# Head sums and the subtraction ahead of the exponent over 1,024 columns, with a shorter warm-up and the last chunk in pieces

## What is computed

```python
x = x + 0.5 * ffn(layernorm(x))
x = x + attention(layernorm(x))
x = x + 0.5 * ffn(layernorm(x))

# ffn: weights with a part that depends on the sequence's first tokens (even and odd rows)
m1 = even[:4] outer odd[:4]; m2 = even[4:] outer odd[4:]       # per sequence
h = gelu(x @ (W1 + scale * m1).T + b1);  out = h @ (W2 + scale * m2).T + b2

# attention: 16 heads of 8 features
def feature_map(x, R):
    x = x / sqrt(8)
    return exp(x @ R - 0.5 * sum(x * x, axis=-1))              # one sum per head
q1, k1 = feature_map(q, R), feature_map(k, R)
kv = k1.T @ v (per head);  z = 1 / (sum(q1) + 1e-8)
out = (q1 @ kv) * z;  return out @ Wo.T + bo
```

## Time and profile before

| what | value |
|---|---|
| median of the runs | 170.91 us |
| the profiled execution's own time | 170.79 us |
| its span, first to last instruction | 169.0 us |
| TensorE, products busy | 160.3 us (95%) |
| TensorE, weight loads busy | 141.7 us (84%) |
| VectorE busy | 136.8 us (81%) |
| ScalarE busy | 124.3 us (74%) |
| GpSimd busy | 83.5 us (49%) |
| share of TensorE in the chain that ended last | 75% |
| share of VectorE in it | 8% |

### The profile page before, as it was taken

How to read it: one execution, slowest core, us unless ns; L and a number is a source line. 1 busy time by engine, 2 the same in 40 slices (tenths; PEclk the granted TensorE clock), 3 DMA queues, 4 the chain that set the end, 5 groups by cost and what they waited for, 6 DMA issues and landing times.

```text
span 169.0 us, 3429 instructions
## 1 busy us (share of the span) xinstructions
PE 160.3 (95%) x1052; PEld 141.7 (84%) x1052; DVE 136.8 (81%) x442; ACT 124.3 (74%) x249; POOL 83.5 (49%) x101
## 2 busy tenths in 40 slices
PE   6997999999999999899999998899999999999993
PEld 6975898989798999577988786788997899899893
DVE  1799988899899948989999999999997679943121
ACT  3299958987968497699959768989898575756320
POOL 5345527319814898948972880882760039100000
PEclk9999999999999999999999999999999999999999
DMA  4990417066430144421331161423236616036403
GB/s 107 321 285 7 127 64 186 22 198 160 170 81 4 64 141 169 132 59 50 138 98 30 64 190 67 113 71 105 87 126 206 189 45 186 2 123 192 124 21 103
DMA packets 31409, 19.55 MB, mean 116 GB/s; under 512 B 2608, under 2 KB 28448, under 8 KB 31392
## 3 DMA queue, kind: packets, MB, share of 16 engines
q1 hardware_dynamic: 31104, 19.34, 38.4%
q10 hardware_dynamic: 288, 0.00, 0.1%
HBM read 11.94 MB, written 7.40 MB: 114 GB/s over the span
## 4 chain that ended last, share of the span: by engine, by line
PE 75%; DVE 8%; ACT 7%; issue 5%; DMA 2%; POOL 1%; DVEq 0%; ACTq 0%; POOLq 0%
PE quad L804 33%; PE quad L788 9%; PE quad L789 8%; PE quad L790 8%; PE quad L821 3%; PE quad L823 3%; PE quad L822 3%; PE ps_t L858 3%; ACT xn L480 3%; PE ps_g L839 2%; DMA scale<-in_rows_dram 2%; ACT gl L520 2%; PE ps_g L804 1%; DVE ex L706 1%; PE ps_r L828 1%
## 5 line engine op out<-in xcount | busy, mean ns | idle before, releaser
L804 PEld LDWEIGHTS quad<-w2e,gl 128*128 128x128 f32 x496 | 60.2, 192 | 3.2 <-ACT gl L520 0.4
L804 PE MATMUL quad<-w2e,gl 128*128 128x128 f32 x496 | 60.8, 275 | 0.0
L520 ACT ACTIVATE gl<-quad,cols 128x512 f32<-128x512 f32 x64 | 42.6, 682 | 16.6 <-PE quad L790 15.5
L411 POOL TENSOR_TENSOR rstd<-veps,mhalf 128x4 f32<-128x4 f32 (+1 forms) x16 | 16.6, 1043 | 29.1 <-DVE veps L132 29.0
L788 PE MATMUL quad<-xh,w1h 128*128 128x512 f32 x64 | 28.5, 445 | 0.4 <-ACT gl L520 0.2
L480 ACT ACTIVATE xn<-X,nmr,rstd 128x128 f32<-128x128 f32 x61 | 25.0, 486 | 3.5 <-DVE nmr L592 3.5
L789 PE MATMUL quad<-xl,w1h 128*128 128x512 f32 x64 | 25.2, 394 | 0.0
L790 PE MATMUL quad<-xh,w1l 128*128 128x512 f32 x64 | 25.2, 393 | 0.0
L432 POOL TENSOR_TENSOR X<-X,b2h 128x512 f32<-128x512 f32 x16 | 20.6, 1305 | 1.1 <-issue 1.1
L690 DVE TENSOR_TENSOR X<-quad,X 128x512 f32<-128x512 f32 (+1 forms) x16 | 10.7, 672 | 11.7 <-PE quad L804 11.7
L788 PEld LDWEIGHTS quad<-xh,w1h 128*128 128x128 f32 x64 | 12.2, 190 | 2.9 <-issue 1.2
(11 more groups left out here) (105 smaller groups left out, 281.6 us busy)
## 6 DMA issues: line engine op xcount, KB each, us to landing
ev<-token_rows SPq DMA_DIRECT2D x7, 512.0 KB, 4.1
folded<-tq SPq DMA_DIRECT2D x12, 256.0 KB, 2.0
land<-folded SPq DMA_DIRECT2D x48, 64.0 KB, 2.2
folded<-atq SPq DMA_DIRECT2D x8, 256.0 KB, 2.0
aland<-folded SPq DMA_DIRECT2D x32, 64.0 KB, 2.1
X<-in_x_dram SPq DMA_DIRECT2D x7, 256.0 KB, 5.5
out_dram<-X SPq DMA_DIRECT2D x7, 256.0 KB, 2.6
w1t<-in_w1t_dram SPq DMA_DIRECT2D x1, 256.0 KB, 3.5
```

Source lines behind the costliest of these rows:

```text
L411: pool.tensor_tensor(rstd[:, i, own], veps[:, i, own], mhalf[:, own], ALU.pow).then_inc(s_rstd, 1)
L520: act.activation(gl[:, f % 2, j], ps_h[j % 2], ACT.Gelu, bias=cols[:, j:j + 1]).then_inc(s_gelu, 1)
L804: ins = pe.matmul(y[:, n * P:(n + 1) * P], gl[:, f % 2, j, n * P:(n + 1) * P], w2e[:, f // PER_B % 2, j], start=(j == 0), stop=(j == HB - 1))
```

## The change

Four things change.

1. VectorE's `head_sums` and `feat` are one instruction each for a whole chunk (1,024 columns) in place of two for its halves. ScalarE's squares and exponents stay in halves. `s_sub` and `s_red` count chunks now. So `head_sums.a` waits for both squares, and `qk.(a+1).0`, `up.8.0` and ScalarE's first exponent wait for the whole `feat.a`.
2. The products ahead of the first data are one group of 11, in `lead`; the groups of 4 and 4 are gone.
3. The last chunk's addition goes in three pieces of 2, 1 and 1 tiles, each from a bank of its own, and the last piece's store is issued by ScalarE's queue.
4. All five strings of `ORDER` are written anew.

```diff
-WARM_UP = (11, 4, 4)
+WARM_UP = 11
+LAST = [slice(0, 2), slice(2, 3), slice(3, 4)]
 ORDER (pe, its first words):
-        "warm_up.0.0 warm_up.0.1 lead.0 select.0 turn.0 warm_up.0.2 select.1 up.0.0 up.0.1 turn.1 up.0.2 up.0.3 "
+        "lead.0 select.0 turn.0 select.1 turn.1 up.0.0 up.0.1 up.0.2 up.0.3 turn.2 up.1.0 up.1.1 down.0.0 down.0.1 "
 ScalarE, feat and exp:
-                    wait(act, s_red, 2 * a + p - 1)
+                    wait(act, s_red, a)
                     act.activation(sq[:, p], halves(p, 0), ACT.Square, scale=0.25).then_inc(s_sq, 1)
-                    act.wait_ge(s_sub, 2 * a + p + 1)
+                    act.wait_ge(s_sub, a + 1)
 VectorE, down of the last chunk:
-                    parts = 2 if f == FC - 1 else 1
+                    for tiles in LAST if f == FC - 1 else [slice(0, NT)]:
+                        dve.wait_ge(s_d, NT * f + tiles.stop)
 VectorE, head sums and feat:
-                    wait(dve, s_sub, 2 * a + p - 1)
-                    dve.wait_ge(s_sq, 2 * a + p + 1)
-                    dve.tensor_reduce(s8[:, p], sq[:, p].rearrange("p u (h d) -> p (u h) d", h=HEADS),
+                    wait(dve, s_sub, i)
+                    dve.wait_ge(s_sq, 2 * i + 2)
+                    dve.tensor_reduce(flat(s8[:]), sq[:].rearrange("p s u (h d) -> p (s u h) d", h=HEADS),
                                       AX.X, ALU.add).then_inc(s_red, 1)
-                    dve.wait_ge(s_red, 2 * a + p + 1)
-                    wait(dve, s_exp, 2 * a + p - 1)
-                    dve.tensor_tensor(heads(ex[:, p]), heads(halves(p, 1)),
+                    dve.wait_ge(s_red, i + 1)
+                    wait(dve, s_exp, 2 * i)
+                    dve.tensor_tensor(heads(ex[:].rearrange("p s u d -> p (s u) d")),
+                                      heads(quad[:].rearrange("p n (k w d) -> p w (n k) d", k=2, w=2)[:, 1]),
 TensorE:
-                    for n in range(WARM_UP[i[1]]):
+                    for n in range(WARM_UP):
                         pe.matmul(ps_h[1][:, 0:P], ident[:], ident[:], start=True, stop=True)
-                            pe.wait_ge(s_sub, 2 * CHUNKS - 1)
+                            pe.wait_ge(s_sub, CHUNKS)
-                        wait(pe, s_sub, 2 * a + n // 2 - 1)
+                        wait(pe, s_sub, a)
 ScalarE, the last store:
+                if stage == "last":
+                    act.wait_ge(s_x3, CHUNKS - 1 + len(LAST))
+                    act.dma_start(chunk_of(out, CHUNKS - 1)[:, LAST[-1]], X[:, CHUNKS - 1, LAST[-1]]).then_inc(s_out, 16)
```

More of the change, by code:

```diff
@@ L279, in wait, with y_of @@
                 eng.wait_ge(s, n)
+        def y_of(f, n):
+            return [ps_y[f % 2], ps_y[f % 2], ps_g, ps_r][n] if f == FC - 1 else ps_y[f % 2]
         def xslot(f):
@@ L375, in _ @@
                     c = i[0] - CHUNKS
-                    parts = 2 if c == CHUNKS - 1 else 1
-                    for h in range(parts):
-                        tiles = slice(NT // parts * h, NT // parts * (h + 1))
+                    for h, tiles in enumerate(LAST[:-1] if c == CHUNKS - 1 else [slice(0, NT)]):
                         sp.wait_ge(s_x3, c + h + 1)
                         sp.dma_start(chunk_of(out, c)[:, tiles], X[:, c, tiles]).then_inc(s_out, 16)
-            sp.wait_ge(s_out, 16 * (CHUNKS + 1))
+            sp.wait_ge(s_out, 16 * (CHUNKS - 1 + len(LAST)))
         @block.gpsimd
@@ L684, in _ @@
                     dve.wait_ge(s_xb, f + 1)
-                    parts = 2 if f == FC - 1 else 1
-                    for h in range(parts):
-                        tiles, part = NT // parts, TOK // parts
-                        dve.wait_ge(s_d, NT * f + tiles * (h + 1))
-                        dve.tensor_tensor(flat(X[:, to, tiles * h:tiles * (h + 1)]),
-                                          (ps_g if h == 1 else ps_y[f % 2])[:, part * h:part * (h + 1)],
-                                          flat(X[:, to, tiles * h:tiles * (h + 1)]), ALU.add).then_inc(
-                            s_x1 if f < CHUNKS else s_x3, 1)
+                    for tiles in LAST if f == FC - 1 else [slice(0, NT)]:
+                        dve.wait_ge(s_d, NT * f + tiles.stop)
+                        dve.tensor_tensor(flat(X[:, to, tiles]), y_of(f, tiles.start)[:, D * tiles.start:D * tiles.stop],
+                                          flat(X[:, to, tiles]), ALU.add).then_inc(s_x1 if f < CHUNKS else s_x3, 1)
@@ L701, in _ @@
                 if stage == "feat":
-                    a, p = i
-                    dve.wait_ge(s_red, 2 * a + p + 1)
-                    wait(dve, s_exp, 2 * a + p - 1)
-                    dve.tensor_tensor(heads(ex[:, p]), heads(halves(p, 1)),
-                                      s8[:, p].rearrange("p (u h) -> p u h", u=4).unsqueeze(3).to_broadcast([P, 4, HEADS, HD]),
+                    dve.wait_ge(s_red, i + 1)
+                    wait(dve, s_exp, 2 * i)
+                    dve.tensor_tensor(heads(ex[:].rearrange("p s u d -> p (s u) d")),
+                                      heads(quad[:].rearrange("p n (k w d) -> p w (n k) d", k=2, w=2)[:, 1]),
+                                      s8[:].rearrange("p s (u h) -> p (s u) h", u=4).unsqueeze(3).to_broadcast([P, 8, HEADS, HD]),
@@ L742, in _ @@
                     pe.transpose(ps_g[:, 0:D], wb[:, 2], ident[:]).then_inc(k_wv, 1)
-                if stage == "warm up":
-                    if i[1] == 0:
-                        pe.wait_ge(k_id, 1)
-                    for n in range(WARM_UP[i[1]]):
-                        pe.matmul(ps_h[1][:, 0:P], ident[:], ident[:], start=True, stop=True)
                 if stage == "turn":
@@ L764, in _ @@
                 if stage == "lead":
+                    pe.wait_ge(k_id, 1)
+                    for n in range(WARM_UP):
+                        pe.matmul(ps_h[1][:, 0:P], ident[:], ident[:], start=True, stop=True)
                     pe.wait_ge(s_xn, 1)
@@ L796, in _ @@
                         if f == CHUNKS:
-                            pe.wait_ge(s_sub, 2 * CHUNKS)
+                            pe.wait_ge(s_sub, CHUNKS)
                         wait(pe, s_x1, min(f - 1, CHUNKS))
                         wait(pe, s_x3, f - 1 - CHUNKS)
-                    y = ps_g if f == FC - 1 and n >= NT // 2 else ps_y[f % 2]
+                    if f == FC - 1 and n == 2:
+                        pe.wait_ge(s_x2, CHUNKS)
+                        pe.wait_ge(m_gs, NB)
+                    y = y_of(f, n)
                     for j in range(HB):
```

1 line of the change is left out of this document (removed), and 110 rows, old and new, of the table ORDER.

## The result

The changed kernel took 185.67 us (two runs, 185.12 and 186.21), the kernel before 170.91. The ratio is 1.088, with a 95% interval from 1.083 to 1.093: 14.8 us slower. The forecast was 181.7, the range 175.5 to 186.5. So the direction and the range were right, and the time lies 4 us above the forecast.

What follows compares the result with a forecast made beforehand. Taken as bound by TensorE in the last layer, with only the attention and first 20 us able to win or lose: 170.8 + 3.8 (start) + 7.4 (attention) - 0.3 (end) = 181.7 us, range 175.5 to 186.5.

Steps and rivals of the forecast that it cites:

- The start, +3.8: First layer: VectorE's and ScalarE's new order delays norms, weights and first products; +3.8 us, bounds +0.5 to +5.5.
- The rival that the start is caught up: VectorE and ScalarE give back by 60 us what they took early at the start; 178.4 us, chance 0.17.
- The chain of a round: Attention: products, second square, whole sum and subtraction run in series; 6.2 us a round, eight rounds +6.0 us.
- +0.3 for fuller rounds: Attention rounds 4 to 6: VectorE's other work, some 4.2 us in the fullest, exceeds its 3.8 us of room; +0.3 us.
- a pause of 3.4 us behind qk.0: Attention, first round: TensorE stays empty for 3.4 us, waiting for the subtraction (line 704).
- the clock's rival: Start and attention: TensorE's pauses bring its clock down, one or two slow rounds and up.0 make +4; 185.7 us, chance 0.13.
- Behind up.8.0 and the end, +0.9 + 0.2 - 0.3: After the attention: moved gram +0.9, mix.3.1 waiting for VectorE +0.2, smaller last addition and store -0.3 us.
- The gram that moved behind up.8.0: End of the attention: a gram that stood ahead of up.8.0 now stands behind it; +0.9 us.
- the eighth round was said to shorten: Attention's last round, 8.50 us before, waited for VectorE's backlog and gets 2.3 us back.
- -0.3 for the smaller last piece: Kernel's end: last addition covers 128 columns in place of 256, with a store of half the size; -0.3 us.
- VectorE's time is what counts: Attention: VectorE's saved time sets the pace, gaining 2.4 us there and 0.3 at the end; 168.1 us, chance 0.06.

Runs made afterwards that it cites:

- kernel of the old start: Changed kernel with the order of the kernel before on all engines up to the attention, short warm-up kept: 181.24 us, ratio 1.060 [1.055, 1.065].
- filled kernel: Changed kernel with unused identity products put into TensorE's idle stretches (8, 3, 14, 9 and 2 of them): 183.81 us, granted clock 1.00.
- the whole instructions alone: Kernel before, in its own order, with only each chunk's sum and subtraction made one instruction each: 181.49 us, ratio 1.064 [1.057, 1.071].

## Why the prediction was right, and where it was off

**The start, +3.8: right, with two wrong places on the way.** qk.0 came 3.76 us late. up.0.0 was said to be at 13.9 and was at 13.19; down.0.0 at 20.7 and was at 19.86. The 2.4 us of work left behind down.0.0 was counted rightly. The rival that the start is caught up fell with the kernel of the old start, which took back all of it. That 3.8 and 3.76 agree so well is partly luck: the filled kernel's qk.0 is at 69.87, so 0.4 of the 3.76 is the clock's, which the forecast did not have in this term, and without it the start is 3.3 us late.

**The chain of a round: right in kind, 0.2 us short.** The forecast summed 6.27 and then called it 6.2 "with the slack of these gaps". The clean rounds are 6.37 on average. The first product to the square took 3.10 us, exactly the 2.44 + 0.66 of the sum, the square 0.61, and the two instructions 1.23 and 1.24 instead of 1.20 and 1.21. The gaps had already been counted once, so to round down for them was the error. Eight rounds of 6.37 are 51.0, +7.4 in place of +6.0. In the clean ones VectorE had time left; the forecast's +0.3 for fuller rounds came in the round of chunk 5 alone, whose sum began 0.3 us late.

**The clock: the term that was mis-sized.** I gave it a chance of 0.13 and left it out of the forecast. It fell in two rounds, which are 1.35 and 1.57 us longer than the clean ones, and in the first layer's first products. That is 2.9 us in the attention; filled pauses gave back 2.85 there and 0.4 at the start. The estimate of "+4" for one or two rounds and a slow up.0 was of the right size. That the time it gave, 185.7, is the one measured is luck: the clock's 3.3 us are less than its 4, and the chain and norm.9, which it did not have, make up for it. What spoke for it was a step of my own working: a pause of 3.4 us behind qk.0 and only 1 us of idle time in each round after it. The measured pauses were 3.70 and, of idle weight loads ahead of qk.2, 2.39. It is not certain in each execution: the whole instructions alone took 180.51 and 180.55 us in two runs with a mean granted clock of 1.000 and 182.43 at 0.991, and the profiled one, at 1.000, has the same pause of 3.70 us behind qk.0. The kernel with the old start took 179.87 us at 1.000, 181.02 at 0.990 and 181.47 at 0.981. So the clock's rival was no alternative to the forecast, but a cost on top of it with a chance of its own. Of the five kernels with a whole subtraction and no filling, four had it in their profiled execution, one of these in a single round.

The Trainium skill ("TensorE: Matmul & The Clock Gate", HAM oscillation) names the pattern: bursts of products, each followed by a wait, and a clock that goes down and up with them; and it advises to order the work so that the engine stays warm. The filled kernel agrees, 2.9 us between the profiled executions. In the page's picture the burst behind a wait starts at the low clock; here qk.1 began at the full one, which fell 1.4 us later. That the same pause leaves the clock alone in some executions is this case's own.

**The round of chunk 5, +1.17: norm.9's 0.9 missed.** The rows of the order showed a pair with nothing between its two parts in the round of chunk 1, and I took it for the pattern of all rounds. In those of chunks 4, 5 and 6 a short instruction stands between them (norm.8, norm.9, odd.4). In that of chunk 4 it took 0.15 us, and the subtraction began 1.26 us after the sum, as without it (1.25). In that of chunk 5 it met GpSimd and cost 0.89. The other 0.28 is the sum that began late. That such an instruction takes 1.0 us beside GpSimd stood in the trace of the kernel before (norm.14), in no row that the prediction read. The Trainium skill ("SBUF — State Buffer", Who interferes with whom) states that a VectorE instruction with two inputs in SBUF contends with a GpSimd instruction that reads SBUF, for ports that one of them locks. The 41 common ends agree. Beside GpSimd's power of four columns, which reads SBUF too, the same instruction took 0.16 us, so here the long GpSimd instructions are the ones that cost.

**Behind up.8.0 and the end, +0.9 + 0.2 - 0.3: +0.30 measured.** The sum was 0.8. The gram that moved behind up.8.0 was counted as a cost. But the eighth round was said to shorten since VectorE's backlog is gone, and the kernel with the whole instructions in the old order, where gram.7 still stands ahead of up.8.0, has no shorter one, 8.75 us. So the 2.1 us that the eighth round gained in the changed kernel were the new order's doing, not the chain's: I had the right sum for a wrong reason. The -0.3 for the smaller last piece was not seen; the kernels with the new end and the short warm-up were no faster than before.

**Together**, from span to span: 3.76 (start) + 7.36 (chain) + 2.92 (clock in the attention) + 1.17 (round of chunk 5) + 0.30 (behind) = 15.5 us. Of the 4.6 us between this and the forecast's 10.9, the clock is 2.9 and norm.9 0.9; the chain is 1.4 more, fuller rounds are as forecast, and what is behind is 0.5 less.

**VectorE's time is what counts: fell.** A whole sum took 1.22 us and two halves 2 x 0.674 = 1.35, so 0.13 us was saved in each of 16 pairs (the subtractions alike), 2.1 us. Its busy time fell by 1.1 (136.8 to 135.7), and the kernel got 15 us longer. That fewer, larger instructions save time was right for the engine and said nothing on the kernel.

## What to carry to other kernels

Before two instructions are made one, ask which buffer the first of them gave back early, and who filled it meanwhile: with four banks in one group, joining the halves turned work of three engines side by side into a chain that runs once per round. Write that chain out link by link, and don't round it down. Where it leaves the matrix engine idle for some us per round, its clock is a cost to be put on top with a chance, not a rival; and look in every round at what the order puts between the links, down to instructions of four columns, and at what GpSimd does beside them.

## What was unexpected of the hardware

- The clock did not fall in the long pause of the attention but about 1.4 us after work had begun again (pause up to 76.61, 0.98 in 77 to 78, 0.50 from 78 on), stayed at 0.50 for 3.4 us while TensorE was busy without a gap, and was back to full for the next pause. The next time it fell 0.5 us after the pause, and in the first layer just as up.0.0 began (0.56 in 13 to 14), so the delay is not a fixed one.
- Executions of one kernel differ with it: 180.5 us at a mean clock of 1.000, 182.4 at 0.991. Once the pauses were filled, all runs lay within 1 us.
- A four-column instruction of VectorE took up to 1.24 us beside a GpSimd instruction of 512 columns instead of 0.15, and all 41 such instructions in thirteen traces ended 0.02 us after GpSimd's.
- Eight identity products fewer at the start gained nothing: the ratio was 1.007 [1.003, 1.011] without them, and 1.004 [1.000, 1.007] with the new end besides, for a reason that no run here found.
